# A fused decoder layer on one core: self-attention on 32-row tiles with two key variants, mask and biases added on TensorE, norms on GpSimd, a new order

## The reference

```python
# x = x + attn(norm(x)); x = x + xattn(norm(x), ctx); x = x + ffn(norm(x))
q, k, v = (heads(x @ W.T + b) for W, b in ...)          # 16 heads of 16
q, k, v = (shift(t, -16) for t in (q, k, v))            # heads 8..15 rolled by 16 rows
scores = einsum('bhgqd,bhgkd->bhgqk', qg, kg) / sqrt(16) # groups of 32 rows
scores = where(causal, -1e9, scores)
out = shift(softmax(scores) @ vg, 16)                   # rolled back
...
q, k, v = proj(Wq, x), proj(Wk, ctx), proj(Wv, ctx)     # 8 heads of 32 columns, over 64 rows
out = proj(Wo, x - softmax(q @ k.T / sqrt(32)) @ v)
...
top2 of x @ gate; out = sum over the two of w * (silu(x @ w0[e]) * (x @ w1[e])) @ wo[e]
```

## Time and profile before

| what | us |
|---|---|
| median of three runs | 453.98 |
| lowest, highest | 452.74, 457.48 |
| the profiled execution | 452.7 |
| its span | 451.3 |
| busy: TensorE, VectorE, ScalarE, GpSimd | 386.2, 286.3, 275.0, 195.5 |

### The profile page before, as it was taken

The page is one execution under the profiler, slowest core; times in us unless marked ns, Lnnn a source line. Parts: engine busy times, 40 slices in busy tenths (PEclk is TensorE's granted clock), DMA queues, the critical chain, the costliest instruction groups (busy, mean ns, idle before and its releaser), DMA issues.

```text
span 451.3 us, 13531 instructions
## 1 busy us (share of the span) xinstructions
PE 386.2 (86%) x4972; PEld 307.5 (68%) x4992; DVE 286.3 (63%) x791; ACT 275.0 (61%) x641; POOL 195.5 (43%) x247
## 2 busy tenths in 40 slices
PE   2779888989789988797653899999999999999994
PEld 1767777678578866675533577777777777777773
DVE  1788688998979998788866044444444544544542
ACT  1738869988458888556400256566566565565662
POOL 3465354534485638744484114224233233233233
PEclk9989899999699999879855899999999999999999
DMA  7821343545254455427356313323323333333312
GB/s 250 301 83 43 117 131 118 155 143 171 76 178 132 143 166 177 143 95 274 126 173 237 94 13 61 58 48 61 60 48 60 60 49 61 58 55 58 54 25 36
DMA packets 38065, 49.56 MB, mean 110 GB/s; under 512 B 4209, under 2 KB 31730, under 8 KB 37746
## 3 DMA queue, kind: packets, MB, share of 16 engines
q1 hardware_dynamic: 29666, 38.12, 26.9%
q0 software_dynamic: 7152, 9.38, 12.2%
q10 hardware_dynamic: 1184, 1.20, 0.8%
HBM read 29.72 MB, written 18.96 MB: 108 GB/s over the span
## 4 chain that ended last, share of the span: by engine, by line
PE 56%; DVE 17%; ACT 9%; POOL 7%; issue 7%; DMA 2%; SPq 0%; DVEq 0%; POOLq 0%; ACTq 0%
PE ps L468 24%; PE ps L485 12%; PE ps L476 4%; ACT FA L526 4%; PE ps L298 3%; DVE STG L746 3%; POOL xs_scratch L952 3%; PE ps L455 2%; PE ps L333 2%; ACT KB2F L542 2%; DMA FA<-in_wpack 2%; PE ps L445 2%; DVE ST L636 2%; ACT VA2F L552 1%; PE ps L370 1%
## 5 line engine op out<-in xcount | busy, mean ns | idle before, releaser
L965 POOL DMA_INDIRECT out<-CTX,VA2F x39 | 60.8, 1558 | 138.9 <-ACT CTX L590 135.9
L876 DVE TENSOR_TENSOR XN2F<-PT,ps 128x512 f32<-128x512 f32 x39 | 26.8, 688 | 59.2 <-PE ps L468 59.2
L468 PE MATMUL ps<-WH,XH 128*128 x156 | 59.6, 463 | 1.4 <-DVE XL L881 1.2
L526 ACT ACTIVATE FA<-ps,WP,CP 128x128 f32<-128x128 f32 x128 | 46.4, 468 | 15.4 <-PE ps L298 10.3
L869 DVE TENSOR_TENSOR GL<-ps,GH 128x512 fp32r<-128x512 f32 x39 | 27.0, 692 | 41.7 <-ACT GH L595 41.7
L468 PE MATMUL ps<-WH,XL 128*128 x156 | 48.7, 393 | 0.0
L606 ACT CAST XH<-ps 128x256 fp32r<-128x256 f32 x39 | 14.6, 374 | 50.4 <-PE ps L455 50.4
L952 POOL DMA_INDIRECT xs_scratch<-XA,IDX x32 | 32.3, 1010 | 17.6 <-issue 17.6
L298 PE MATMUL ps<-FA,WP 128*128 128x128 f32 x256 | 36.8, 304 | 3.6 <-DMA FA<-in_wpack 2.5
L298 PEld LDWEIGHTS ps<-FA,WP 128*128 128x128 f32 x256 | 34.5, 217 | 6.1 <-issue 4.4
L590 ACT ACTIVATE CTX<-ps,WS 128x256 f32<-128x256 f32 x39 | 18.5, 475 | 29.7 <-DVE WS L864 25.5
(11 more groups left out here) (150 smaller groups left out, 955.0 us busy)
## 6 DMA issues: line engine op xcount, KB each, us to landing
STG<-in_w SPq DMA_DIRECT2D x32, 256.0 KB, 3.4
lo_scratch<-STG SPq DMA_DIRECT2D x48, 128.0 KB, 1.8
VA2F<-xs_scratch SPq DMA_DIRECT2D x39, 130.0 KB, 2.1
STG<-in_wo SPq DMA_DIRECT2D x16, 256.0 KB, 2.9
CTX<-in_ctx SPq DMA_DIRECT2D x16, 128.0 KB, 2.3
out<-XF SPq DMA_DIRECT2D x16, 128.0 KB, 2.8
XF<-lo_scratch SPq DMA_DIRECT2D x4, 512.0 KB, 6.6
FA<-lo_scratch SPq DMA_DIRECT2D x1, 2048.0 KB, 8.1
```

What stands on the lines that cost most here:

```text
L468: ins = t.matmul(bk, x_[:, k, :], w_[:, bass.ds(eoff[j] + k * MLP, MLP)], start=(n == 0 and k == 0), stop=(n == 2 and k == 1))
L526: ins = a.activation(KP[:, c, h, :], PS[:, B_KK, c * 128:(c + 1) * 128], ACT.Identity, bias=WP[:, o:o + 1], scale=cp(C_MASK4 + h, 1))
L876: v.tensor_tensor(GG[:, j % 2, :], SG[:, j % 2, :], PS[:, 3 + 2 * (j % 2), :], ALU.mult).then_inc(S["gg"], 1)
L965: p.indirect_dma_start(out, bass.IndirectOffsetOnAxis(XG[:, j % 6, 259:260].bitcast(U32), 0), Y[:, j % 3, :], None, compute_op=ALU.add).th ...
```

## The change

The expert loop keeps its instructions. The front is rewritten:

- Projections are made from plain transposes only. `xt` writes each sequence's 64 columns and then its first 16 again, so that rolled heads read columns 16 to 79 of it. Biases enter as bf16 matmuls of a selector (SELB) with three bf16 parts of the bias (BR); `qk`, `vp` replace `qkv`. The value matmuls are 64 columns of the array wide, two for each one before.
- Keys have two masked variants (even and odd heads of a pair) in place of four, written by `ke`; `s1` is 32 matmuls on array tiles of 32x32, in four PSUM banks, on top of four bf16 matmuls that add the mask. `m1` (VectorE) takes the maximum and subtracts it straight from PSUM; `mask` and `sub` go.
- `os` writes the rolled heads beside, and SP copies them back to their rows by four SBUF DMAs a tile (step `un`); `xa` on GpSimd adds all 256 columns; `xb` goes.
- In the second block keys, queries and values are copied by plain full copies (`kve`, `q2e`); `s2` is 16 matmuls on 32x64 tiles in the same four banks as `s1`, `pv2` 16 on 64x64 tiles.
- Norms: VectorE adds EPS, GpSimd takes the root and makes the normalized rows (`nx0`, `nx1`, `nx2`). GpSimd also makes 40 of the 48 weight remainders.
- The stream is a ring of eight tiles; the remainders of w0 stay in SBUF, so 32 pieces are stored and two loads of 2 MB bring them back; the last groups have three tiles and one.
- All five lists of steps are new.

```diff
-GROUPS = ((0, 4), (4, 4), (8, 4), (12, 2), (14, 2))
+LO_POOL = frozenset(n for n in range(48) if n % 6 != 5)
+GROUPS = ((0, 4), (4, 4), (8, 4), (12, 3), (15, 1))
-B_TR, B_KK, B_QV, B_S1, B_PV, B_UN, B_KQ2, B_V2, B_S2, B_T2, B_PV2, B_WO, B_T3, B_LG, B_RK = (
-    0, 1, 2, 3, 5, 0, 6, 7, 5, 0, 7, 1, 6, 2, 2)
+B_S = 0
+B_TR, B_QK, B_V, B_PV, B_KV, B_Q2, B_T2, B_PV2, B_WO, B_T3, B_LG, B_RK = 4, 4, 6, 5, 6, 4, 5, 6, 5, 4, 5, 6
...
 ORDER_SP = """
...
-ld:45 ld:46 out:11 wl:0 sv:44 wl2:2 sv:45 out:12 sv:46 out:13 ld:47 sv:47 out:14 out:15 wl:1 wl2:3"""
+ld:38 ld:39 out:10 un:13 ld:40 ld:41 un:14 ld:42 ld:43 out:11 un:15 ld:44 ld:45 ld:46 wl:1 out:12 wl:2 ld:47 out:13
+out:14 out:15"""
...
+            def qk(i):
...
+                for j in range(4):
+                    c, at_ = j % 2, PS[:, B_QK, j * 128:(j + 1) * 128]
+                    t.matmul(at_, BR[:, j * 128:(j + 1) * 128], SELB[:, :], start=True, stop=False)
+                    for k in range(2):
+                        o = k * 512 + j * 128
+                        ins = t.matmul(at_, WQK[:, o:o + 128], XT[:, i % 2, k, :, 16 * c:16 * c + 64], start=False,
+                                       stop=(k == 1))
...
+            def vp(i):
...
+                for c in range(2):
+                    at_ = PS[:, B_V, c * 128:(c + 1) * 128]
+                    t.matmul(at_, SELB[:, :], BR[:, 512 + c * 128:640 + c * 128], start=True, stop=False)
                     for k in range(2):
+                        for b in range(2):
+                            ins = t.matmul(at_[64 * b:64 * b + 64, :], XT[:, i % 2, k, b, 16 * c:16 * c + 64],
+                                           WV[:, k, c * 128:(c + 1) * 128], start=False, stop=(k == 1))
...
             def s1(i):
...
+                for r in range(4):
+                    t.matmul(PS[:, B_S + r, 0:128], IDB[:, :], flat(MASKB[:, :, :]), start=True, stop=False)
                 for c in range(2):
                     for w in range(4):
+                        for r in range(4):
+                            p_, n_ = slice(32 * r, 32 * r + 32), slice(32 * w, 32 * w + 32)
+                            ins = t.matmul(PS[n_, B_S + r, c * 64:(c + 1) * 64], QT[p_, i % 2, c, n_],
+                                           KM[p_, i % 2, :, c, n_], start=False, stop=(c == 1))
...
+            def kv(i):
...
+                for b in range(2):
+                    for u in range(2):
+                        q = slice(64 * b, 64 * b + 64)
+                        ins = t.matmul(PS[64 * u:64 * u + 64, B_KV + b, 0:128], WX[q, 256 + 64 * b:320 + 64 * b],
+                                       CTX[q, i % 3, 128 * u:128 * u + 128], start=True, stop=True)
...
             def s2(i):
...
+                        for r in range(4):
+                            p_, n_ = slice(32 * r, 32 * r + 32), slice(64 * b, 64 * b + 64)
+                            ins = t.matmul(PS[n_, B_S + r, c * 64:(c + 1) * 64], QT2[p_, i % 2, c, n_],
+                                           KT2[p_, i % 2, c, n_], start=True, stop=True)
...
             def xt(i):
...
+                a.copy(XT[:, i % 2, :, :, 0:64], src)
+                a.copy(XT[:, i % 2, :, :, 64:80], src[:, :, :, 0:16]).then_inc(S["xt"], 1)
...
+            def ke(i):
...
+                for h in range(2):
+                    ins = a.activation(flat(KM[:, i % 2, h, :, :]), PS[:, B_QK, 256:512], ACT.Copy,
+                                       scale=cp(C_MASK2 + h, 1))
...
+            def less_max(i, s1, m, src, heads, done):
+                step(v.tensor_reduce(m, src, AX, ALU.max))
+                settle()
+                v.tensor_tensor(s1, src, bc(m.rearrange("p (r c) -> p r c", r=4), 3, 512 // heads),
+                                ALU.subtract).then_inc(S[done], 1)
...
+            def normed(dst, i, k):
+                pw.wait_ge(S["rs", k], i + 1)
+                pw.wait_ge(S["half"], 1)
+                p.tensor_tensor(RS[:, i, k, 1:2], RS[:, i, k, 0:1], HALF[:, :], ALU.pow).then_inc(S["pool"], 1)
                 made[0] += 1
                 pw.wait_ge(S["pool"], made[0])
+                return p.tensor_scalar(dst, X[:, i % 8, :], MV[:, i, k, 0:1], RS[:, i, k, 1:2], ALU.subtract, ALU.mult)
...
             def xa_(i):
                 pw.wait_ge(S["os"], i + 1)
+                pw.wait_ge(Q["un", i % 2], 64 * (i // 2 + 1))
...
+            def un(i):
+
+                sw.wait_ge(S["os"], i + 1)
+                for b in range(0, 128, 64):
+                    for to, of, n in ((16, 0, 48), (0, 48, 16)):
+                        s.dma_start(OS[b + to:b + to + n, i % 2, 1, :], OS[b + of:b + of + n, i % 2, 2, :]
+                                    ).then_inc(Q["un", i % 2], 16)
```

More of the change, by code:

```diff
@@ L221, in program @@
         S = {n: sem("s_" + n) for n in (
[L222 to L223 removed]
+            "zero half sel ones mb br pad dve pool xn tr xt qk qt kt vp va s1 m1 exp pt pv os xa xn2 kv kt2 va2 q2 qt2 "
+            "s2 m2 e2 t2 pt2 pv2 ao df wo x3 xn3 t3 xt3 lg l cho rk ex idx tok wh lo lop cnt tab rev te warm "
             "ut xh xb2 xl h0 h1 sg gg gt gh gb gl y ws yw").split()}
```

675 lines of the change are left out of this document (318 added, 357 removed).

## The result

The change made the kernel slower: 471.07 us median (470.44 to 472.69, 4 runs) against 454.36 us for the kernel before in the same session, a ratio of 1.0365 with a 95% interval of 1.0303 to 1.0427. The prediction was 435.0 us, faster, with a range that ends at 456. On a second chip the ratio was 1.039 (1.029 to 1.050). The profiled execution took 471.1 us, with a span of 469.7.

The account below looks back on a forecast made before the run. No engine was full; the loop's start at 254.2 us decided. Last pv 201.4 + 6.5 - 14.5 - 3 = 190.4, xa:15 4 later, drain 42: loop at 236.5, 17.7 earlier, so 452.7 - 17.7 = 435.0 us, range 414 to 456.

Parts of the forecast that it names:

- TensorE's work, +6.5 us: Up to the last pv: TensorE's added and removed passes net +0.4 us a tile at full clock, over 16 tiles.
- the price of a change of array shape: TensorE, up to the last pv: 0.12 us each, six more per tile, +0.72 us a tile.
- - 14.5 for its idle time: Up to the last pv: half of TensorE's idle time goes, since VectorE and ScalarE lose 20 to 30% of their work.
- - 3 for the clock: Up to the last pv: TensorE's clock recovers a quarter of the 13 us that full speed would be worth.
- The start of the drain: From the last pv to xa:15: 4 us, for VectorE, four SBUF copies and their landing, so xa:15 at 194.5 us.
- the drain: From xa:15 to the expert loop's start: 23 us to xn3:15 plus 19 behind it, 42 us against 51 before.
- GpSimd's normalization at 0.5 us: In the front on GpSimd: 48 normalizations of 128x256 at 0.5 us, the middle of 0.222 and 0.732, 24 us in all.
- (1): Up to the last pv: TensorE's idle time stays, for want of free PSUM bank slots; 452.5 us, no change; chance 0.21.
- (2): Up to the last pv: idle time and clock come back nearly whole, - 25 and - 9; 418 us; chance 0.17.
- (3): In the front: GpSimd becomes the bound by its SBUF lock with VectorE; 462 us; chance 0.12, shared with dearer small passes.
- dearer small passes: On TensorE in the front: small passes cost more than priced, over 457 us; chance 0.12, shared with (3).
- signs of being wrong: New profile: GpSimd normalization over 0.75 us, eviction waits over 15, copy waits well over 4 a tile, TensorE busy off over 15.

Follow-up runs that it names:

- e3: Changed kernel without the bf16 bias and mask matmuls (so it lacks bias and mask): 473.4 us, 1.028 of the kernel before.
- e15: Changed kernel with probabilities times values as 16 matmuls of 136 columns instead of 64 of 17, the step about as long: 447.9 us, 0.982 of the kernel before.
- e16: Kernel before with probabilities times values as 16 matmuls of 136 columns instead of 64 of 17: 452.5 us, 0.995 of the kernel before.
- e12: Changed kernel with only TensorE's step order changed, so that steps with many short passes stand apart: 507.0 us, 1.107 of the kernel before.
- e13: Changed kernel with about as many TensorE steps moved as in e12, but short-pass steps not spread apart: 522.8 us, 1.141 of the kernel before.
- e9: Kernel before with probabilities times values as 16 matmuls of 68 columns instead of 64 of 17: 451.8 us, 0.992 of the kernel before.
- e11: Kernel before with 27 of the 48 normalizations moved to GpSimd: 462.0 us, 1.016 of the kernel before.
- e1: Changed kernel with the 48 normalizations back on VectorE: 479.7 us, 1.046 of the kernel before.
- e2: Changed kernel with the normalizations and two thirds of the weight remainders on VectorE: 486.2 us, 1.062 of the kernel before.

## Why the prediction was wrong

Up to the last pv the forecast was 190.4 us and the trace has 218.4. Of these 28.0 us, the work is 1.6, idle time 8.8 and the clock 17.6. The other 8 came behind it. By its own steps:

- **TensorE's work, +6.5 us: right.** It was +8.1. The pitch of 32x32 passes (9.9 ns for s1, 10 taken) and the bf16 passes (14.6 us for 160 in e3, 0.09 each, 0.08 taken) were near enough; the price of a change of array shape was not measured alone. The upper bound of its own terms is +1.5 us a tile and not +1.2 (V at 0.120 alone adds 0.96), and no run shows that small passes at the end of a step overlap with nothing. GpSimd, ScalarE, VectorE: up to the loop ScalarE fell by 49 us (43 forecast) and VectorE by 41 (35, of which the priced terms give only 28).
- **"- 14.5 for its idle time": the first step that failed.** The idle time for other engines did fall, by 22.2 us, more than I gave it. But 16.5 us of a new kind came: waits for TensorE's own instructions. The prediction counted passes by their pitch and never their number against the packets in which the program arrives: it put that wait at nothing. Net -5.7.
- **"- 3 for the clock": the second, wrong in sign and the larger miss.** It was +14.6. In e15, with the same work and nearly no such waits, the clock's cost is 10.8, below the 12.2 of the kernel before. So both terms go with one edit: a fourth as many pv passes, of the same length in sum. Whether the gaps lowered the clock or the many short passes, e15 can't tell, as its passes are longer too. Longer pv passes where there are hardly any such gaps give back only 1.4 us (e16), which speaks for the gaps, though there was less to win there (12.2 us in all). In the changed kernel more idle time came with more of this cost (e3, e12, e13), in the kernel before it didn't (e9, e11). The cause of the lower clock stays open.
- **The start of the drain** (4 us from the last pv to xa:15) was 8.4 (218.4 to 226.8), **the drain** 45.3 us in place of 42: sizes, 8 us together.
- **GpSimd's normalization at 0.5 us** was 1.22, outside my bounds (0.222 to 0.732) and far over the 0.43 of the estimate beside them, 35 us more over 48, and GpSimd was busy 193.8 us up to the loop. It wasn't the bound (e1), but it is among what TensorE waits for once the instructions come in time (e15).
- **The rivals.** (1) expected idle time to stay, for want of bank slots; but the waits on ScalarE and VectorE, which empty the banks, are 1.4 us at most in the rows of after. (2) had the size of what other engines give back. (3) GpSimd as the bound is refuted by e1 and e2; by its own rows its longest times add up to about 230 us and not 240, so it priced no more than rival 1. The time fell where rival 3 and dearer small passes had 0.12, but by neither. The true mechanism wasn't among them.
- **The signs.** Two of the signs of being wrong came: the normalization over 0.75 us, and TensorE's busy time off by over 15 us. It is up by 22.7 to the last pv, but 14.6 of that is the clock and not the small passes that the sign named.

With instructions in time and the clock that goes with it, the changed kernel would have been the faster one: e15 comes to 447.9 us, 1.8% under the kernel before, though not to 435 (it computes something else in pv, at the same length). A version with the whole result that beats the kernel before was not found; fewer and longer matmuls in pv need another layout of the probabilities, which wasn't tried.

## What to carry to other kernels

Cutting a step into small tiles multiplies instructions, not only columns: count matmuls and weight loads, compare with the packets of the instruction queue in the DMA view, and see how many of them a crowded stretch needs. An idle time put down to "issue" in the middle of a run without waits is the sign. Then fewer, longer matmuls are worth more than shorter ones: e15 gained over 20 us with no work taken out, e3 nothing with 15 us taken out. TensorE's clock is a term of its own, and here it was the larger part of the loss: split a stretch into work, clock and idle before explaining it.
